# A recurrent two-layer kernel: every step placed one by one, and the second experts' first bias added by ScalarE

## The reference

```python
xn = _layernorm(x)
s  = _L0_attn_ref(xn, ...)          # q, k, v; softmax(q k^T / 128) with the diagonal masked; times v
g  = _silu(_L0_ffn_ref(xn, ...))    # 8 experts, 128 -> 256 -> 128, top 2 by a softmax gate
x  = x + s * g
xn = _layernorm(x)
s  = _L1_attn_ref(xn, ...)          # Mamba block: in_proj, causal conv of 4 taps, silu, x_proj,
                                    # softplus delta, selective scan with 16 states, out_proj
g  = _silu(_L1_ffn_ref(xn, ...))    # 8 experts, 128 -> 512 -> 128, one per token by a centroid
x  = x + s * g
```

## Time and profile before

| | |
|---|---|
| median of 3 runs | 1081.34 us (1081.3 to 1081.43) |
| the profiled execution | 1082.32 us, span from first to last instruction 1080.4 us |
| mean granted TensorE clock | 0.925 |
| first scans of the eight batches | 155.8, 276.0, 398.7, 520.7, 643.8, 765.9, 889.0, 993.3 us |
| groups present | ramp A, H; batches 0 to 5 all; batch 6 without A; batch 7 only F and the scan |

### The profile page before, as it was taken

How to read it: one execution, slowest core, us unless ns; L and a number is a source line. 1 busy time by engine, 2 the same in 40 slices (tenths; PEclk the granted TensorE clock), 3 DMA queues, 4 the chain that set the end, 5 groups by cost and what they waited for, 6 DMA issues and landing times.

```text
span 1080.4 us, 16900 instructions
## 1 busy us (share of the span) xinstructions
PE 925.1 (86%) x5056; PEld 619.7 (57%) x5056; DVE 850.3 (79%) x1635; ACT 598.3 (55%) x1107; POOL 562.2 (52%) x501
## 2 busy tenths in 40 slices
PE   5979879997799959997799959998799957894994
PEld 3644556765566635765567636765467735552671
DVE  4245767899878988799878889799888896988974
ACT  3324536567465746567465656567465654655551
POOL 0010105548464675548564584548654586668654
PEclk9988889999899989999699989999699988887997
DMA  8100001111111121111101121111201121102211
GB/s 275 41 20 1 20 30 40 47 40 56 59 39 48 42 64 39 57 40 57 59 31 47 37 79 40 51 37 58 67 30 48 35 71 59 54 30 69 78 64 30
DMA packets 60856, 56.52 MB, mean 52 GB/s; under 512 B 6290, under 2 KB 47746, under 8 KB 60258
## 3 DMA queue, kind: packets, MB, share of 16 engines
q1 hardware_dynamic: 58722, 51.25, 14.3%
q0 software_dynamic: 2048, 4.20, 1.2%
HBM read 19.58 MB, written 12.78 MB: 30 GB/s over the span
## 4 chain that ended last, share of the span: by engine, by line
PE 59%; DVE 20%; issue 8%; POOL 5%; ACT 5%; DMA 2%; SPq 1%; DVEq 0%; POOLq 0%; ACTq 0%
PE work L699 9%; PE work L705 9%; PE work L738 7%; PE yacc L772 6%; DVE st L1218 6%; PE work L747 5%; PE work L628 3%; DVE acc L1103 3%; PE work L649 2%; POOL st L1393 2%; PE work L613 2%; PE work L736 2%; PE b_row L763 2%; DVE b_row L1211 2%; PE work L676 1%
## 5 line engine op out<-in xcount | busy, mean ns | idle before, releaser
L1393 POOL TENSOR_TENSOR st<-st,Cs 128x512 f32<-128x512 f32 x249 | 319.3, 1287 | 317.8 <-DVE st L1218 241.0
L855 ACT ACTIVATE dA<-delta,Aneg 128x512 f32<-128x512 f32 x256 | 178.3, 712 | 11.3 <-DVE st L1218 11.0
L772 PE MATMUL yacc<-st,w_ident 128*128 128x512 f32 x256 | 144.1, 647 | 28.1 <-POOL st L1393 20.0
L1218 DVE TENSOR_TENSOR_SCAN st<-dA,dbu 128x512 f32<-128x512 f32 x128 | 154.9, 1210 | 4.3 <-ACT dA L855 3.8
L1218 DVE TENSOR_TENSOR_SCAN st<-dA,b_row 128x512 f32<-128x512 f32 x123 | 148.9, 1211 | 2.2 <-POOL y L1400 1.5
L705 PEld LDWEIGHTS work<-w_w2a,hid 128*128 128x128 f32 x1024 | 123.3, 194 | 29.9 <-issue 15.2
L738 PE MATMUL work<-xsT,hs 128*128 128x128 f32 x704 | 136.9, 318 | 0.0
L855 ACT ACTIVATE hid<-work,w_b1a 128x512 f32<-128x512 f32 x128 | 87.8, 686 | 84.4 <-PE work L699 84.4
L1400 POOL TENSOR_TENSOR y<-y,st 128x512 f32<-128x512 f32 x105 | 133.5, 1272 | 0.6
L699 PE MATMUL work<-xnT,w_w1a 128*128 128x512 f32 x256 | 128.8, 604 | 5.3 <-DVEq L1108 2.3
L705 PE MATMUL work<-w_w2a,hid 128*128 128x128 f32 x1024 | 128.1, 279 | 0.4 <-DVEq L1108 0.4
(11 more groups left out here) (200 smaller groups left out, 1404.0 us busy)
## 6 DMA issues: line engine op xcount, KB each, us to landing
hs<-w_w1f SPq DMA_DIRECT2D x88, 256.0 KB, 2.3
xs_in<-xs_dram SPq DMA_DIRECT2D x16, 256.0 KB
ys_dram<-ys SPq DMA_DIRECT2D x16, 256.0 KB, 2.4
x_in<-in_x_dram SPq DMA_DIRECT2D x8, 256.0 KB, 2.8
w_w1f<-in_w1f_dram SPq DMA_DIRECT2D x1, 2048.0 KB, 8.2
w_w2f<-in_w2f_dram SPq DMA_DIRECT2D x1, 2048.0 KB, 12.7
kept_dram<-x_tok SPq DMA_DIRECT2D x8, 256.0 KB, 2.5
xr<-kept_dram SPq DMA_DIRECT2D x8, 256.0 KB
```

The lines of the kernel that those rows point to most:

```text
L772: mm(yacc[:], ident[:], state(s), start=False, stop=(n == NS - 1)).then_inc(sig["y_sum0"], 1)
L855: return nc.scalar.activation(out, in_, func, **k)
L1218: V.tensor_tensor_scan(state(s), dA[:, s % DECAYS], (dbu0, rows_bank(n, b))[h][:], 0.0, ALU.mult, ALU.add).then_inc(sig["scan"], 1)
L1393: G.tensor_tensor(state(s), state(s), Cs[:, n % 2], ALU.mult).then_inc(sig["P"], 1)
```

## The change

`ROWS` now has a line for every step of every engine, the scan work too (group S: `b` the B row, `d` decays, `p` products, `e` sums of the second half, `a` sums of the first, `c` the C rows), and a group P for the preparation of weights. A place is a share of the batch; `WARP` bends the places of some batches. `program(engine)` sorts all steps of all batches into one list per engine, which is walked once; there are no iterations, slots or ramp order any more, only DVE's scans stand at fixed numbers. In the resulting order of TensorE, all H steps of batch 0 stand before `xT` of batch 1; the 64 one-column beta matmuls stand behind that `xT`. In the middle batches `b 0`, `c 0`, `xs 0` and `h 0` stand before `b 1`, and `xs 1`, `h 1` behind it. On SyncE `w 0` and `w 1` stand before `xin`. `ln0` and `ln1` are split into `ln0`/`xn` and `ln1`/`xm`, with their own statistics tiles, and in the middle batches there is a scan between the two parts of the first and three between those of the second; `o` is split in four on TensorE; `sc` gives up `al`. The output DMA is a step of its own (`out`). In the last batch DVE adds x in place of POOL. Banks of the last steps are taken modulo 2.

```diff
-        hs = sb("hs", [128, 2, H1])
+        hs = sb("hs", [128, 2, H1 + HC])
...
+def program(engine):
+    if LAG[engine] is None:
+        return ORDER
+    steps = []
+    for t, k, b in PLACES:
+        r = ROWS[k]
+        late = place(r[0], b, (math.floor(r[3] * STEPS) + r[LAG[engine]]) / STEPS)
+        steps.append((round(late * STEPS, 3), t, k, (r[0], r[1:3], b)))
+    if engine == "dve":
+        steps += [(b * STEPS + i, -9.0, i, ("S", ("scan", i), b)) for b in range(NB) for i in range(STEPS)]
+    return [x[3] for x in sorted(steps)]
...
                         if k >= 2:
-                            filled(sp, g, ("h", k - 2), b)
+                            emptied(sp, g, ("h", k - 2), b)
...
-                            sp.dma_start(w1s[:, k % 2], W["w1f"][:, bass.ds(e * H1, H1)]).then_inc(w_ld[k % 2], 16)
+                        sp.dma_start(w1s[:, k % 2], W["w1f"][:, bass.ds(e * (H1 + HC), H1 + HC)]).then_inc(w_ld[k % 2], 16)
...
                     for c in range(HC):
-                        r = w[:, c * 128:(c + 1) * 128]
-                        mm(r, b1p[:, c * 128:(c + 1) * 128], sel_b[:, bass.ds(e, 1)].broadcast_to([96, 128]),
-                           start=True, stop=False)
-                        last = mm(r, w1s[:, i % 2, c * 128:(c + 1) * 128], xsT[:, i // 4 % 2, i % 4 * 128:(i % 4 + 1) * 128],
-                                  start=False, stop=True)
+                        last = mm(w[:, c * 128:(c + 1) * 128], w1s[:, i % 2, c * 128:(c + 1) * 128],
+                                  xsT[:, i // 4 % 2, i % 4 * 128:(i % 4 + 1) * 128], start=True, stop=True)
...
                 for e in range(E):
-                    last = mm(yacc[0:96], betaM[:, e * 96:(e + 1) * 96], W["w1f"][:, e * H1:(e + 1) * H1],
-                              start=(e == 0), stop=(e == E - 1))
+                    for c in range(HC):
+                        k = e * (H1 + HC) + c * 128
+                        last = mm(yacc[:, e * HC + c:e * HC + c + 1], W["w1f"][:, k:k + 128], W["betaT"][:, e:e + 1],
+                                  start=True, stop=True)
...
+                elif name == "o" and i == NT - 1:
+                    filled(act, g, step, b)
+                    act.wait_ge(sig["rs"], b.of(1, 1))
+                    since(act, sig["out"], b.of(16, -32))
+                    for t in range(NT):
+                        last = go(s_tok[:, t], w[:, t * 128:(t + 1) * 128], ACT.Copy, scale=rs[:, t:t + 1])
+                    last.then_inc(fr, 1)
...
+                elif name == "xi":
+                    filled(act, g, step, b)
+                    k = i * TAPS + TAPS - 1
+                    go(cv[:, i], w[:], ACT.Identity, scale=W["conv_w"][:, k:k + 1], bias=W["conv_b"][:, i:i + 1]
+                       ).then_inc(sig["cv_a"], 1)
...
-                    go(hsT[:, i % 2], w[:], ACT.Relu).then_inc(fr, 1)
+                    for c in range(HC):
+                        last = go(hsT[:, i % 2, c * 128:(c + 1) * 128], w[:, c * 128:(c + 1) * 128], ACT.Relu,
+                                  bias=w1s[:, i % 2, H1 + c:H1 + c + 1])
+                    last.then_inc(fr, 1)
...
-                    lk[g](V.tensor_scalar(cv[:, i], w[:], cw[:, k:k + 1], W["conv_b"][:, i:i + 1], ALU.mult, ALU.add))
...
             def first_bias():
-                own(V.tensor_tensor(W["b1r"], yacc[0:96], W["b1r"], ALU.add))
-                split(W["b1r"], b1p, H1)
+                b1 = W["w1f"][:].rearrange("p (e k) -> p e k", e=E)[:, :, H1:H1 + HC]
+                own(V.tensor_tensor(b1, b1, yacc[:, 0:E * HC].rearrange("p (e k) -> p e k", e=E), ALU.add))
```

More of the change, by code:

```diff
@@ L210 @@
-AHEAD = {"A": 2, "H": 1, "F": 0, "C": -1}
-def groups_of(it):
-    return "".join(g for g in "AHFC" if 0 <= it + AHEAD[g] < NB)
-def slots(groups, engine):
-    out = [[] for _ in range(STEPS)]
-    for t, k in PLACES:
-        g, s = ROWS[k][0], ROWS[k][1:3]
-        if g in groups:
-            late = 0 if engine == "pe" else LATER[engine][g, s]
-            out[max(0, min(STEPS - 1, int(t * STEPS) + late))].append((g, s))
-    return out
-JOBS = {g: [s for gg, s in ORDER if gg == g and (g, s[0]) not in NO_BANK] for g in "AHFC"}
@@ L229 @@
-BANK = {(r[0], r[1:3]): r[8] for r in ROWS if r[8] is not None}
-SPARE = 3
-assert BANK["C", ("op", 0)] < SPARE - 1 and all(BANK["F", x] < SPARE - 1 for x in JOBS["F"])
-assert all([j for j in ORDER if BANK.get(j) == k][-1][0] != "C" for k in range(BANKS))
-IN_BANK = {g: [[s for s in JOBS[g] if BANK[g, s] == k] for k in range(BANKS)] for g in "AHFC"}
-LINKS = {("dve", "A"): 32, ("dve", "H"): 48, ("pool", "A"): 2, ("pool", "H"): 8}
[259 rows of a table added]
+]
+WARP = {
[10 rows of a table added]
+}
+AHEAD = {"A": 2, "H": 1, "S": 0, "F": 0, "C": -1, "P": 0}
@@ new lines, with place @@
+LAG = {"pe": None, "sp": None, "act": 4, "dve": 5, "pool": 6}
+SPARE = 3
+def place(g, b, x):
+    points = WARP.get((g, b))
+    if points is None:
+        return x + (b - AHEAD[g])
+    k = 0
+    while k + 2 < len(points) and x > points[k + 1][0]:
+        k += 1
+    (x0, y0), (x1, y1) = points[k], points[k + 1]
+    return y0 + (x - x0) * (y1 - y0) / (x1 - x0)
+PLACES = sorted((place(r[0], b, r[3]), k, b) for k, r in enumerate(ROWS) for b in range(NB if r[0] != "P" else 1))
+ORDER = [(ROWS[k][0], ROWS[k][1:3], b) for _, k, b in PLACES]
@@ new lines @@
+BANK = {(r[0], r[1:3]): r[7] for r in ROWS if r[7] is not None}
+TAKEN_AT = {("A", ("o", 0)): ("o", NT - 1)}
+READY = {}
+EMPTY = {}
+BEFORE = {}
+LAST_IN = {}
+for _g, _s, _b in ORDER:
+    if (_g, _s) in BANK:
+        READY[_g, _s, _b] = 1 + sum(1 for g, s, b in READY if g == _g)
+    _job = _g, TAKEN_AT.get((_g, _s), _s), _b
+    if _job[:2] in BANK and _job not in EMPTY:
+        _k = bank_of(*_job)
+        EMPTY[_job] = 1 + sum(1 for j in EMPTY if j[0] == _g and bank_of(*j) == _k)
+        BEFORE[_job] = LAST_IN.get(_k)
+        LAST_IN[_k] = _job
@@ L448, in row_of, with bank, free_of @@
             return sel_b[:, n:n + 1].broadcast_to([96, 128])
-        def bank(g, step):
-            return work[BANK[g, step]]
+        def bank(g, step, b):
+            return work[bank_of(g, step, b.n)]
+        def free_of(g, step, b):
+            return free[g][bank_of(g, step, b.n)]
         def tiles(ap):
@@ L568, in _ @@
+            load_x(Batch(0))
             for part, names in LOADS.items():
@@ L575, in _ @@
                 sp.dma_start(xs_dram[4 * k:4 * k + n].rearrange("i p d -> p i d"), fe[:, 0:n]).then_inc(sig["xs_zero"], 16)
-            run(sp, body)
+            for g, step, n in program("sp"):
+                do(g, step, Batch(n))
             sp.wait_ge(sig["out"], 16 * NB)
@@ L679, in a_step @@
                     last = expert_step(step, b)
-                if last is not None and (g, name) not in NO_BANK:
+                if last is not None and (g, step) in BANK:
                     last.then_inc(ready[g], 1)
@@ L687, in expert_step @@
                     return None
-                w = bank(g, step)
+                w = bank(g, step, b)
                 if name == "b2":
@@ new lines, in do @@
+                    a_step(g, step, b)
+                elif g == "F" or name == "c":
+                    f_step(g, step, b)
+                elif g == "S" and name == "b":
+                    spread(i, b)
+                elif g == "S" and name == "a":
+                    add_state(i, b)
+                elif g == "S" and name == "e" and b.is_(NB - 1):
+                    add_second(i, b)
+                elif g == "C" and name == "op":
+                    project(g, step, b)
+                elif g == "P" and name == "pe":
+                    beta_products()
@@ L843, in beta_products @@
                 last.then_inc(prep_pe, 1)
-            def weights_wait():
-                pe.wait_ge(prep_dve, 4)
-            early = {(-2, "A", ("silu", 0)): beta_products}
-            run(pe, body, weights_wait)
+            for g, step, n in program("pe"):
+                do(g, step, Batch(n))
         @block.scalar
@@ L1003, in decay_rates @@
                 go(Aneg[:], W["alog"][:], ACT.Exp).then_inc(prep_act, 1)
-            def prepare():
-                act.wait_ge(prep_dve, 5)
             act.wait_ge(loads["small"], 16 * len(LOADS["small"]))
             go(bqs[:], W["bq"][:], ACT.Copy, scale=1.0 / D)
-            early = {(-2, "A", ("silu", 0)): decay_rates}
-            run(act, body, prepare)
+            for g, step, n in program("act"):
+                do(g, step, Batch(n))
         @block.vector
@@ L1234, in c_step @@
                     since(dve, sig["out"], b.of(16))
-                    r = tiles(bank("C", step)[:])
+                    r = tiles(bank("C", step, b)[:])
                     V.tensor_tensor(r, r, xn1_tok[:, par], ALU.add).then_inc(sig["opx"], 1)
@@ L1331, in _ @@
             V.memset(ones8[:], 1.0)
-            V.memset(betaM, 0.0).then_inc(prep_memset, 1)
```

(8 more changed lines are left out.)

635 lines of the change are left out of this document (254 added, 381 removed), and 400 rows, old and new, of tables (ROWS, WARP, sig).

## The result

The changed kernel took 1045.15 us (median; runs from 1042.03 to 1049.58), the kernel before on the same chip 1081.32. The ratio is 0.9673, interval 0.9641 to 0.9706: 36 us, 3.3% faster. The profiled execution took 1042.03 with a span of 1040.2, against 1080.4, so the trace has 40.2 us to explain. Predicted were 1042 and a span of 1041.3.

What follows compares the result with a forecast made beforehand. TensorE bounds a middle batch's first phase, VectorE its end and border. Gains of 42.6 (six middle batches), 3 (batch 6) and 3.5 (batch 7), less 10 for the ramp, give 39.1 off: 1042.2 us, range 1014 to 1064.

Steps and rivals of the forecast that it cites:

- The bias: Second experts' first product: four bias matmuls fewer per token tile save 0.39 us, nine of eleven tiles counting, 3.5 per batch.
- The conv product: Conv's first product leaves VectorE, 807 ns twice per batch, in TensorE's phase where VectorE has slack: 0 in middle batches.
- Splitting the norms: A scan fills VectorE's wait for GpSimd's power in the first normalisation: 2.1 us per batch; the second's wait counts 0.
- The border: Between batches, token tiles and expert step 0 run inside TensorE's 5.00 us wait: 1.5 us per batch, between 0 and 2.6.
- Four Relus: ScalarE, per token tile: four Relus with bias replace one, 1.26 us together, 7.3 more per batch, hidden by TensorE's phase.
- The slower rival: ScalarE's 10.1 us more per batch reach the path by over two thirds, middle batches gain nothing: 1095 us, chance 0.11.
- The ramp: Before the first scan: batch 0's H steps precede batch 1's transposes, making batch 1's x 6 to 17 us later; 10 taken.
- The beta matmuls: In the ramp, 64 one-column matmuls behind batch 1's transposes, no longer in shadow: 7.4 to 14.8 us.
- The two conv rounds: In the ramp, batch 0's H chain: two conv rounds in one bank, through tanh and gate, 11.4 us after 2.3 of copies.
- the rates, 2 to 3: In the ramp, the last piece of batch 0's H chain before batch 1's transposes, taken as 2 to 3 us.
- Batch 7: Last batch, held to be TensorE-bound: shorter expert steps save 4.3 us at most, 3.5 taken.
- the marks that I named: Expected signs: expert step 0.97, four Relus 1.26, first scan 162 to 172, batches 115 apart, norm wait at most 0.7, step before row spread.

Runs made afterwards that it cites:

- bias alone: Kernel before, own order, bias matmuls of the second experts' first product removed, four Relus with a fixed bias column: 1072.22 us, ratio 0.9936.
- order alone: Changed kernel with the bias matmuls back on TensorE (of zeros) and one Relu per token tile: 1071.41 us, ratio 0.992.
- two repairs: Changed kernel with the beta matmuls early again: 1031.29 us; with batch 1's attention and batch 0's Mamba steps also alternated in the ramp, old banks: 1020.68 us.

## Why the prediction was right, and where it was not

*The bias.* The price, 0.39 per tile from the row, was a little low: 0.44 to 0.46 (0.89 against 1.33 to 1.35), and 0.33 - 0.22 = 0.11 per chunk. The chip gave 29.8 for the matmuls, 4.7 per middle batch against my 3.5: all eleven steps count (11 x 0.44 = 4.8), past the 4.3 that I had kept as a bound. The Trainium skill, "TensorE: Matmul & The Clock Gate", section "Step-by-step: what each phase is for", says that weight loads are pulled ahead beside a running matmul. My estimate from it, that only the streaming (56 ns each) would come back, was 2.0 per batch; the 0.11 per chunk and the 4.7 per batch decide against that estimate here. What I did not see is that the price holds in the new order only. In the old one the same edit gives a quarter of it: TensorE full in seven windows out of twelve said what it did, not that a shorter step would be passed on. Why it is not passed on is shown in part only (the wait for four Relus).

*VectorE.* The conv product, priced at 0, cost 0.5 per middle batch and 8.5 in the medians: both engines are near 103 of 113.5, and the slack of VectorE that I had counted on is gone. Splitting the norms was predicted at 2.1 per batch and is worth 3.3. The waits for the powers fell from 17.3 and 27.2 to 6.3 and 3.3.

*The border.* I took 1.5 of 0 to 2.6 and reasoned that VectorE bounds there. It measured 2.7, just past my upper bound, with 3.2 us more at half clock in the first section, and another 7.3 in batch 7, where I had not looked. Single prices now add to 4.7 + 3.3 + 2.7 + 0.5 = 11.2 against 8.2 gained per batch: they overlap.

*ScalarE.* Four Relus in 1.14 (predicted 1.26), 81.7 us busy per batch (84), worth 2.5 in the medians, which is within the spread. The slower rival, from 7.1 per batch on, was far off; in the old order the same Relus cost 4.3 in all, of which TensorE's wait behind them is 0.7 per batch in the middle section.

*The ramp.* This is the step that failed in size: it was priced at 10 and measured 22.6, and its top of 17 was passed too. The beta matmuls were inside their range (13.65, range 7.4 to 14.8). Batch 1's transposes came 7 to 10 later than worked out, though x of batch 0 was ready 4.0 earlier than before (62.96 against 66.98). I had 22 to 25 us from batch 0's hidden-state transposes to batch 1's; it took 36.0 (70.98 to 107.00). The two conv rounds were right (14.1 for 13.7) and B and C took 7.7 (5.8 to 7.4). Then I had only "the rates, 2 to 3", where the trace has a chain of 12.4 through TensorE, VectorE and GpSimd: 3.0 for the places of the tokens, 4.6 until GpSimd has issued three scatters, 1.4 for the power, and 3.4 for VectorE's scaling and the delta that frees the bank. The centroid products, 1.9 at half clock, were left out as well. I had followed TensorE's queue and not GpSimd's and VectorE's. From the gate logits to x of batch 1 it took 176.05 - 121.42 = 54.6, as predicted (56.6 or some 4 less). The long serial stretch ran at half clock to its end:

```profile
77.60:132.20 54.60, 37.84 (x123) 24.47 (x124) 23.11 (x70) 15.90 (x26) 5.47 (x6) 0.50 0.03 10
```

The clock rule of the Trainium skill, same page, section "What's actually happening" (the throttled state is the default, activity releases it), agrees with this 0.50 behind the idle stretches from 60 us on (11.50 ahead of the transposes at 70.98), and with the ramp's 0.92 once the steps alternate.

*Batch 7* gave 10.5 for 3.5: the matmuls alone are worth 6.9 there (83.5 with them), at a granted clock of 0.98 against 0.95, where 11 x 0.44 would be 4.8.

Of the marks that I named, the batches' length (113.0 to 117.7 for 115), the Relus and the step ahead of the row spread came true; the norm's wait is gone from the middle batches, but the ramp has one of 4.86; the step was shorter than 0.97, and the first scan at 178.4 lay outside 162 to 172.

## What to carry to other kernels

Price a removed instruction twice, in the schedule it leaves and in the one that it enters: here bias alone gave 8 us, order alone 9, both 36. When a list is reordered, follow every engine's queue through the fill of the pipeline too; the steady state hid some 24 us of ramp that two repairs took back, down to 1020.7. And where an engine waits at a border, try the work that is ready in front of the wait: here, putting it back behind cost 19 us. When a total comes out right, check its terms: here four misses cancelled.

## What the runs showed of the hardware

Removing 352 matmuls recorded with 81.3 us of busy time took only 26.7 us off TensorE's busy time in the old order (925.1 to 898.4). Time at half clock is not equally dear everywhere: in scans 0 to 12 of a batch of the kernel before, 7.8 us more of it go with 1.0 us more in length, in those of the changed kernel 8.5 to 9.8 more go with 4.0 to 4.6. Batch 4 has a second stretch at half clock in the changed kernel and in both ramp variants, and takes 117.7 or 117.8 us where its neighbours take 113.0 to 113.7; with one Relu it is 114.7. The runs of the changed kernel spread by 7.5 us, those of the kernel before by 2.1 beside them and by up to 5.4 later. What starts that stretch was not settled.
